# Six weight slots instead of five, combine weights turned behind the expert loop, and logits in two bank pairs

## The reference

```python
def _L0_ffn_ref(x, phi, scale, w1, b1, w2, b2):
    xn = _l2norm(x, axis=2)
    phin = scale * _l2norm(phi, axis=0)
    logits = jnp.einsum('bmd,dnp->bmnp', xn, phin)
    d = jax.nn.softmax(logits, axis=1)
    b_, m_, n_, p_ = logits.shape
    c = jax.nn.softmax(logits.reshape(b_, m_, n_ * p_), axis=-1).reshape(b_, m_, n_, p_)
    xs = jnp.einsum('bmd,bmnp->bnpd', xn, d)
    h = jax.nn.gelu(jnp.einsum('bnpd,ndh->bnph', xs, w1) + b1[None, :, None, :], approximate=False)
    ys = jnp.einsum('bnph,nhd->bnpd', h, w2) + b2[None, :, None, :]
    y = jnp.einsum('bnpd,bmnp->bmd', ys, c)
    return y
```

## Time and profile before

| | us |
|---|---|
| time before, median of 3 runs | 987.24 (986.78 to 992.46) |
| profiled execution, its own time | 988.6 |
| span of the profile, first to last instruction | 986.7 |
| TensorE busy (matmul) | 863.3 |
| VectorE busy | 454.2 |
| ScalarE busy | 316.0 |
| GpSimd busy | 280.2 |

### The profile page before, as it was taken

One profiled execution on the slowest core, in us unless ns is written; L12 is line 12 of the kernel. 1 busy time (PEld: TensorE's weight loads), 2 busy tenths in 40 slices (PEclk: granted clock), 3 DMA queues, 4 the chain that ended last, 5 costly groups with the idle time before them and its releaser, 6 DMA issues. The chain is left out here.

```text
span 986.7 us, 17884 instructions
## 1 busy us (share of the span) xinstructions
PE 863.3 (87%) x6209; PEld 631.3 (64%) x6209; DVE 454.2 (46%) x1520; ACT 316.0 (32%) x904; POOL 280.2 (28%) x242
## 2 busy tenths in 40 slices
PE   6899999889999999884997999977465999999991
PEld 6787878666556656553854777757463666666661
DVE  6764565538633333221655688836782222222220
ACT  2544434127533323221032566633101221221210
POOL 1540000000000000000233355530018488888444
PEclk9999999779899999997997899975555999999996
DMA  8999000000069999987500000001105344455222
GB/s 265 274 337 378 1 2 2 1 1 1 2 260 422 420 421 421 420 341 171 179 15 1 1 2 0 1 1 38 39 14 149 78 105 99 92 105 105 40 24 25
DMA packets 60311, 129.52 MB, mean 131 GB/s; under 512 B 26350, under 2 KB 42336, under 8 KB 50640
## 3 DMA queue, kind: packets, MB, share of 16 engines
q1 hardware_dynamic: 30288, 119.20, 33.6%
q0 software_dynamic: 29952, 9.36, 6.9%
HBM read 116.35 MB, written 11.98 MB: 130 GB/s over the span
## 5 line engine op out<-in xcount | busy, mean ns | idle before, releaser
L1806 POOL DMA_INDIRECT out_dram<-yr,put x48 | 105.7, 2203 | 58.8 <-issue 36.0
L1261 POOL MEMSET xg<- 96x74 f32 x1 | 0.2, 157 | 412.0 <-PE bank L1234 412.0
L1870 PE MATMUL bank<-zTa,w 128*128 128x372 f32 x256 | 90.4, 497 | 0.8 <-DVE zTb L1944 0.8
L1793 POOL DMA_INDIRECT zr<-z_rows,take x48 | 66.7, 1389 | 85.7 <-issue 85.7
L1953 DVE TENSOR_TENSOR hT<-sg,bank 128x372 f32<-128x372 f32 x64 | 31.8, 538 | 108.1 <-ACT sg L1914 63.1
L1177 PE MATMUL bank<-w2s,eg 128*64 128x192 f32 x768 | 69.4, 330 | 5.7 <-ACT cT L1088 5.7
L1870 PEld LDWEIGHTS bank<-zTa,w 128*128 128x128 f32 x256 | 47.5, 194 | 38.2 <-ACT sg L1914 8.4
L1109 DVE COPY eh<-bank 128x384 f32<-128x384 f32 x32 | 17.8, 557 | 107.7 <-PE bank L1153 107.7
L1884 PE MATMUL bank<-w2r,hT 128*124 128x192 f32 x384 | 66.1, 329 | 0.8 <-DVE hT L1953 0.8
L1177 PEld LDWEIGHTS bank<-w2s,eg 128*64 128x64 f32 x768 | 56.2, 137 | 14.2 <-issue 11.5
L1914 ACT ACTIVATE sg<-bank 128x372 f32<-128x372 f32 x64 | 27.3, 478 | 116.0 <-PE bank L1875 116.0
(11 more groups left out here) (287 smaller groups left out, 1727.3 us busy)
## 6 DMA issues: line engine op xcount, KB each, us to landing
w1s<-in_w_dram SPq DMA_DIRECT2D x32, 1152.0 KB, 12.8
w2s<-in_w_dram SPq DMA_DIRECT2D x32, 1152.0 KB, 13.7
w<-in_w_dram SPq DMA_DIRECT2D x8, 1024.0 KB, 8.2
xt<-in_x_dram SPq DMA_DIRECT2D x22, 336.0 KB, 8.0
xT<-in_xT_dram SPq DMA_DIRECT2D x22, 333.0 KB, 7.3
ys<-eo SPq DMA_DIRECT2D x64, 48.0 KB, 9.6
w2r<-in_w2r_dram SPq DMA_DIRECT2D x8, 384.0 KB, 4.1
w1s<-ys SPq DMA_DIRECT2D x6, 432.0 KB, 8.6
```

What stands on the lines that cost most here:

```text
L1793: nc.gpsimd.indirect_dma_start(zr[b][:, j, :], None, z_rows, bass.IndirectOffsetOnAxis(ap=take[:, k:k + 1], axis=0), bounds_check=NROW - 1 ...
L1806: nc.gpsimd.indirect_dma_start(rows_out, bass.IndirectOffsetOnAxis(ap=put[:, k:k + 1], axis=0), yr[e % 2][:, j, :], None, bounds_check=OUT ...
L1870: nc.tensor.matmul(bank[to + 2 * part + half][:, 0:HS], w13[b][:, 0, at:at + 128], zTa[b][:, half * HS:(half + 1) * HS], start=True, stop= ...
```

## The change

It has six parts.

1. **Six slots** (RING = 6). Only slots 0 and 1 (EARLY = 2) lie in memory that is free from the start; slots 2 to 5 lie in two tiles `w1l` and `w2l` that take the place of attention's buffers and weights, and their first loads wait for attention's last residual (`sp.wait_ge(s_h, 2 * T)`). For that `cb` is split: attention's part stays, the rest (phi, image marks, hidden biases) is a second table `cd`, loaded right behind it.
2. **Combine weights behind the loop.** Eight buffers `cw` (CB = 8); the expert loop spreads the first eight tiles, DVE spreads the other 14 behind it. All transposes and ACT's copies stand behind the loop, in banks 0 to 3; combine's products use banks 4 to 7. `cT` lies in the memory of slots 4 and 5.
3. **Four output buffers** (EOB = 4) instead of two.
4. **Last outputs straight into combine's rows.** Pairs 0 to 26 (DIRECT = 27) are stored to `ys` as before. The outputs of pairs 27 to 31 go from `eo` straight to their places in `e1` and `e2`, six DMAs a pair, each from 21 or 22 rows of `eo` to one row of `e1` or `e2`. The rows of pairs 0 to 26 are collected from `ys` by six DMAs of 27 rows each, issued behind the direct stores of pair 28. Combine has one wait for all of them, and no groups of tiles.
5. **Images turned by one place.** Image marks are rotated so that image 63 lies where the loads of whole rows put it.
6. **Logits in two bank pairs.** Even tiles use banks 1 and 2, odd tiles 6 and 7; logits of tile t wait for the exponentials of tile t-2.

```diff
-RING = 5
-EARLY = 3
+RING = 6
+EARLY = 2
+EOB = 4
+DIRECT = 27
...
+CTN = 20
+CB = 8
...
+        w1s = [sb(f"w1s{q}", [128, 3 * HID]) for q in range(EARLY)]
+        w2s = [sb(f"w2s{q}", [128, 2, HB, ED]) for q in range(EARLY)]
...
+        w1l = sb("w1l", [128, RING - EARLY, 3 * HID])
+        w2l = sb("w2l", [128, RING - EARLY, 2, HB, ED])
...
+        e1 = w1l[:, 0:2].rearrange("p s (t d) -> p (s t) d", d=ED)
+        e2 = w2l[:, 0:2].rearrange("p s e j d -> p (s e j) d")
+        cTs = [w1l[:, 2:4].rearrange("p s n -> p (s n)"), w2l[:, 2].rearrange("p e j d -> p (e j d)")]
...
             sp.dma_start(cb[:], ins["cb"]).then_inc(s_cbi, 16)
+            sp.dma_start(cd[:], ins["cd"]).then_inc(s_cbi, 16)
             sp.dma_start(cc[:], ins["cc"]).then_inc(s_cci, 16)
...
             def logits(t, q):
                 b = q % 2
                 pe.wait_ge(s_hTc, T + t + 1)
-                if after(t, 1):
-                    pe.wait_ge(s_cce, t)
-                    pe.wait_ge(s_cdl, t)
+                if after(t, 2):
+                    pe.wait_ge(s_cce, t - 1)
+                    pe.wait_ge(s_cdl, t - 1)
                 for c in range(2):
-                    nc.tensor.matmul(bank[1][0:TP, 0:NE], hnT[b][:, c, :], phin[:, c, :], start=(c == 0), stop=(c == 1))
+                    nc.tensor.matmul(bank[1 + 5 * b][0:TP, 0:NE], hnT[b][:, c, :], phin[:, c, :], start=(c == 0), stop=(c == 1))
...
                     if s == EARLY:
-                        sp.wait_ge(s_h, T)
+                        sp.wait_ge(s_h, 2 * T)
...
                 p = s - RING
                 if p >= 0:
-                    b = p % 2
+                    b = p % EOB
                     sp.wait_ge(s_do, p + 1)
                     for e in range(2):
-                        sp.dma_start(ys_of[p + e * NPAIR], eo[b][e * B:(e + 1) * B]).then_inc(s_eo[b], 16)
-                if s == NPAIR + 1:
-                    sp.wait_ge(s_dh, NPAIR - 1)
+                        n = p + e * NPAIR
+                        if p < DIRECT:
+                            sp.dma_start(ys_of[n], eo[b][e * B:(e + 1) * B]).then_inc(s_eoo[b], 16)
+                        else:
+                            for to, lo, hi in places(n):
+                                sp.dma_start(to, eo[b][e * B + lo:e * B + hi]).then_inc(s_eoo[b], 16)
+                if p == DIRECT:
+                    sp.dma_start(e2[NE:2 * NE, 0:T], ins["b2"].rearrange("n (t d) -> n t d", d=ED)).then_inc(s_el, 16)
+                if p == DIRECT + 1:
+                    for r in range(DIRECT - EOB, DIRECT):
+                        sp.wait_ge(s_eoo[r % EOB], rows_out_by(r))
                     for k in range(2):
-                        sp.dma_start(e2[k][NE:2 * NE], ins["b2"].rearrange("n (t d) -> n t d", d=ED)).then_inc(s_b2, 16)
+                        n = slice(k * NPAIR, k * NPAIR + DIRECT)
+                        for g in range(2):
+                            to = slice(g * NE + k * NPAIR, g * NE + k * NPAIR + DIRECT)
+                            sp.dma_start(e1[to, 0:T - 1], ys_of[n, g * (T - 1):(g + 1) * (T - 1)]).then_inc(s_el, 16)
+                        sp.dma_start(e2[n, 0:T], ys_of[n, 2 * (T - 1):B]).then_inc(s_el, 16)
+
+        def places(n):
+            return ((e1[n:n + 1, 0:T - 1], 0, T - 1), (e1[NE + n:NE + n + 1, 0:T - 1], T - 1, 2 * (T - 1)), (e2[n:n + 1, 0:T], 2 * (T - 1), B))
...
-                if 1 <= s < T + 1:
-                    spread_c(s - 1)
+                if 1 <= s <= CB:
+                    spread_c(dve, s - 1)
...
-                if p < T:
-                    pe.wait_ge(s_eTa, p + 1)
-                elif p >= 2:
+                if p >= 2:
                     pe.wait_ge(s_do, p - 1)
...
+        def combine_act(act):
+            for t in range(T):
+                act.wait_ge(s_eT, t + 1)
+                nc.scalar.copy(cT(t), bank[t % 4][:, 0:2 * TP].rearrange("p (c q) -> p c q", c=2)).then_inc(s_eTa, 1)
...
         def combine_pe(pe):
-            pe.wait_ge(s_b2, 32)
+            for part in range(2):
+                pe.wait_ge(s_dc[part], NPAIR)
+
+            def transpose_c(t):
+                pe.wait_ge(s_ecw, t + 1)
+                if t >= 4:
+                    pe.wait_ge(s_eTa, t - 3)
+                spread = cw[t % CB][:].rearrange("p g n -> p (g n)")
+                nc.tensor.transpose(bank[t % 4][:, 0:TP], spread[:, 0:128], ident[0:TP, 0:TP])
+                nc.tensor.transpose(bank[t % 4][:, TP:2 * TP], spread[:, 128:4 * NE], ident[0:TP, 0:TP]).then_inc(s_eT, 1)
+
+            for t in range(T):
+                transpose_c(t)
+            pe.wait_ge(s_el, 16 * (1 + 2 * GB))
+            for b in range(EOB):
+                pe.wait_ge(s_eoo[b], rows_out_by(NPAIR - EOB + b))
+            pe.wait_ge(s_db, NPAIR)
+            pe.wait_ge(s_do, NPAIR)
+            pe.wait_ge(s_eTa, T)
```

More of the change, by code:

```diff
@@ L164, in tower @@
         open_scope()
+        colD, nD = columns(PACK_D)
+        cd = sb("cd", [128, nD])
+        Dc = {name: of(cd, colD, name) for name in colD}
+        xy = sb("xy", [128, 2, NE, B])
+        phisq = sb("phisq", [HALF, 2, NE])
+        ce = sb("ce", [TP, T, NE])
+        image = Dc["image"][:, 0:GB]
+        image_or_any = Dc["image"]
+        w1s = [sb(f"w1s{q}", [128, 3 * HID]) for q in range(EARLY)]
+        w2s = [sb(f"w2s{q}", [128, 2, HB, ED]) for q in range(EARLY)]
+        b1s = Dc["b1s"].rearrange("p (e n j) -> p e n j", e=2, n=NPAIR)
+        open_scope()
         colB, nB = columns(PACK_B)
@@ L212, in tower @@
         open_scope()
-        w1s += [sb(f"w1s{q}", [128, 3 * HID]) for q in range(EARLY, RING)]
-        w2s += [sb(f"w2s{q}", [128, 2, HB, ED]) for q in range(EARLY, RING)]
-        open_scope()
         ha = [sb(f"ha{b}", [TP, 3, 2, 64]) for b in range(2)]
@@ L231, in tower @@
         close_scope()
+        close_scope()
+        open_scope()
+        w1l = sb("w1l", [128, RING - EARLY, 3 * HID])
+        w2l = sb("w2l", [128, RING - EARLY, 2, HB, ED])
+        w1s += [w1l[:, q] for q in range(RING - EARLY)]
+        w2s += [w2l[:, q] for q in range(RING - EARLY)]
         open_scope()
@@ L409, in tower @@
         s_yc = [sem("routed_output_copied_act"), sem("routed_output_copied_dve")]
-        s_eo = [sem(f"expert_output_out{b}") for b in range(2)]
+        s_eoo = [sem(f"slot_output_out{b}") for b in range(EOB)]
         s_ph = sem("norm_constants_steps")
@@ L441, in tower @@
         s_eTa = sem("combine_weights_kept")
-        s_b2 = sem("expert_output_bias_in")
-        s_el = [sem(f"expert_rows_in{k}") for k in range(len(LOADS))]
+        s_el = sem("expert_rows_in")
         s_ey = sem("combine_product")
@@ L882, in dispatch_act @@
             act.wait_ge(s_ln, 5 + 4)
-            nc.scalar.activation(hnorm[:], hvar[:], ACT.Sqrt, scale=float(ED)).then_inc(s_cns, 1)
+            nc.scalar.activation(hnorm[:], hvar[:], ACT.Sqrt, scale=float(ED)).then_inc(s_phs, 1)
             def copy_T(t, q):
@@ L896, in exps @@
                     act.wait_ge(s_ccw, t - 1)
-                nc.scalar.activation(cexp[b][:], bank[1][0:TP, 0:NE], ACT.Exp, bias=cneg[b][:], accum_out=csum[b][:]).then_inc(s_cce, 1)
+                nc.scalar.activation(cexp[b][:], bank[1 + 5 * b][0:TP, 0:NE], ACT.Exp, bias=cneg[b][:], accum_out=csum[b][:]).then_inc(s_cce, 1)
                 act.wait_ge(s_cdl, t + 1)
@@ L906, in store @@
                     if isinstance(t, int) and t == T - 1:
-                        last = nc.scalar.copy(xy[:, c, :, B - 1:B].rearrange("p n g -> p g n"), p[:, c, 0:1])
+                        last = nc.scalar.copy(xy[:, c, :, B - 1:B].rearrange("p n g -> p g n"), p[:, c, GB - 1:GB])
                     else:
@@ L1081, in output @@
                 act.wait_ge(s_dy, p + 1)
[L1082 to L1088 removed]
+                if p >= EOB:
+                    act.wait_ge(s_eoo[p % EOB], rows_out_by(p - EOB))
+                nc.scalar.copy(eo[p % EOB][:], bank[6 + b][:, 0:ED]).then_inc(s_do, 1)
             for s in range(NPAIR + 2):
@@ L1223, in combine_pe @@
         def combine_pe(pe):
[L1224 removed]
+            for part in range(2):
[15 more added lines that the diff above has]
+            pe.wait_ge(s_eTa, T)
             def product(t):
[L1227 to L1228 removed]
                 if t >= 4:
                     pe.wait_ge(s_h, 2 * T + t - 3)
[L1231 to L1234 removed]
+                nc.tensor.matmul(bank[4 + t % 4][0:TP, 0:ED], cT(t)[:, 0], e1[:, t, :], start=True, stop=False)
+                nc.tensor.matmul(bank[4 + t % 4][0:TP, 0:ED], cT(t)[:, 1], e2[:, t, :], start=False, stop=True).then_inc(s_ey, 1)
             for t in range(T):
```

107 lines of the change are left out of this document (33 added, 74 removed).

## The result

The changed kernel takes 982.77 us (median of 20 runs, 975.87 to 988.55), the kernel before in the same comparison 990.7 us. The ratio is 0.9939, 95% interval 0.9917 to 0.9961: 0.6% faster, 6 us, where the forecast was 970 us and 17 us. The ratio leaves out executions over 1.5% above a kernel's fastest one, so it is not the quotient of the two medians. The profiled execution took 982.76 us (span 980.9), 5.8 us less in span than the one before.

The account below looks back on a forecast made before the run. It took full DMA engines to bound the experts and busy TensorE dispatch, with idle time at dispatch's start and behind the experts. 988.6 - 6.8 (dispatch) - 10.5 (gap, 5.8 of it the slot) = 971.3, on the median's scale 970 us; range 962 to 982.

Parts of the forecast that it names:

- Dispatch: Start of dispatch: two bank pairs shorten the logits' wait and keep the clock at 1.00; 6.8 us, bounds 1.8 and 6.8.
- rival 1: Start of dispatch: the clock falls all the same, only 1.8 of 6.8 us are gained; 975 us, chance 0.20.
- Six slots: Experts: one weight pair less streams through the full DMA queue, late loading costs nothing; 5.8 us.
- the gap: From last expert product through combine: combine ends at 470.1 instead of 480.6, 10.5 us, of which 5.8 are the slot.
- Turning the weights: Behind the experts: 22 ACT copies take 7.8 us, output copy and first transposes 0.4; done at 451.3.
- SP's queue: Behind the experts: 30 issues at 0.596 us take 17.9 us, at least 1.8 to land; done at 452.4.
- Rival 3: Behind the experts: SP's issues take longest and the gap gives back the slot's gain; 983.6 us, chance 0.10.
- The transfers: Behind the experts: biases 4.8 us and collecting loads 11.9 us at 223 GB/s land last, at 454.2.
- rival 2: Collecting loads: 27 partitions reach 7 of 16 parts, 184 GB/s, 14.4 us, 2.5 us more; 972.5 us, chance 0.10.
- Three lines: Before the first combine product: weight turning (451.3), SP's issues (452.4) and transfers (454.2); only the last to end counts.
- Half clock: Start of combine: after some 3 us idle the first three tiles run at half clock, 2.0 us more.

Follow-up runs that it names:

- e1: The kernel before with only the logits in two bank pairs changed; ratio to the kernel before 0.9931 (0.9887 to 0.9974).
- e2: The changed kernel without the six collecting loads; direct stores landed 2.1 us behind the last issue instead of 8.7.
- e3: The changed kernel without the 30 direct stores; 18.1 us from the collecting loads' first issue to the first combine product.
- e4: The changed kernel with 28 rows a piece instead of 27 and 24 direct stores instead of 30; 980.75 us.
- e5: e4 with the two collecting loads onto partitions 64 and above issued by ACT; loads at 184 GB/s, first product 22.0 us behind the last expert product.
- e8: The changed kernel with 29 rows a piece instead of 27; 1072.62 us.
- e10: The changed kernel with 120 more TensorE products between the last turned weight and the wait for the collecting loads; 989.92 us.
- e6: The changed kernel with all six collecting loads issued on ACT's queue, direct stores alone on SP's; 976.01 us.
- e7: e6 with 28 rows a piece and 24 direct stores; 983.2 us.

## Why the prediction was wrong

- **Dispatch** (forecast 6.8 us): right, 6.7 in the trace of the change, 6.8 (2.6 to 11.2) by time alone in e1. The granted clock stayed 1.00 through these turns, so rival 1 falls.
- **Six slots** (5.8 us): right. The experts end 12.3 us earlier; less 6.7 leaves 5.6. Measured by itself, from the first hidden product to the end of the last output, the stage took 179.1 us before and 173.2 after, 5.9 less; in e2, e3, e4, e5, e8 and e10, whose loops differ in the last pairs alone, it took 172.3 to 173.8. The first hidden product before, and after:

```profile
269.81 2.73 PE L1149 MATMUL bank<-w1s,xy 128*64 128x384 f32 x8 [0.48 <-ACT xy L907]
```

```profile
263.37 2.66 PE L1177 MATMUL bank<-w1s,xy 128*64 128x384 f32 x8 [0.48 <-ACT xy L923]
```

The late loads were through in the slices of dispatch, 40 us before that product. The slots alone weren't tried, since their memory is that of the weights now turned in the gap, so what left the loop shares in this number. That the experts ended within 0.3 us of the forecast 436.3 is luck in part: dispatch's first logits came at 195.5 to 206.7 us in the runs with the same code up to there.

- **Turning the weights** (7.8 us and 0.4): 5.6 us, from 436.57 to 442.2. Too dear, but it was not last.
- **SP's queue** (17.9 us at 0.596 us an issue): a direct store takes 0.75 us, SP also waited 3.0 us ahead of the loads for the stores that they read, for which the line had no term, and alone it ends 13.2 us behind the experts (e2), where the forecast had 452.4 - 443.1 = 9.3. Too cheap, but not last either. Rival 3 gave 983.6 us for this line, less than 1 us from the result, but by a cause that e2 rules out. (Its "6.8 us stay" is a slip: its own times, 483.8 against 480.6, leave 3.6, and 983.6 is 987.24 less 3.6.)
- **The transfers**: the step that failed. It had two faults. The prediction put the collecting loads at 223 GB/s, the rate of 64-row loads, "11.9" us; they ran at 183, and from issue to product they need 18.1 us (e3). That was the rate of rival 2, 184 GB/s, which had a chance of 0.10. (In the proportion of the two rows that it names, 223 GB/s onto 64 partitions would have made 94 onto 27; its 7 of 16 parts come from the port count that it cites.) Landing at 451.4, 14.8 us behind the experts, they would have cost 3.7 us more than the forecast's 11.1.
- The second fault is larger: "Three lines now end before the first combine product, and the last of them counts". The lines are not independent, and the line of the transfers had no term for the direct stores. The 18 direct stores of the last pairs stand in SP's queue and on the same DMA engines behind 2.65 MB of loads; when these are all but through, some 0.2 MB of small packets are still to move. Without the loads the same stores land 2.1 us behind their issue (e2), with the loads in another queue they still move behind them (e6). That is 7.2 us more (458.5 against 451.4), and together 22.0 us to the first product instead of 11.1.
- **Half clock** (2.0 us): 2.6 us (e10). Right in kind; the wait before it was 16 us, not the 3 of the forecast.

The sum: forecast 17.3 us, of which dispatch and slots gave 12.3 instead of 12.6, and the gap took 7.3 instead of giving 4.7.

## What to carry to other kernels

A maximum over lines holds only where the lines use different resources: where two of them end in the same DMA queue or engines, ask what each issue stands behind, and add. Loads of 27 rows moved 183 GB/s with a DMA share of 0.57, where 128-row loads of the weights move 420; so try one load of all 128 rows, with its rows arranged in DRAM for that, before filling a tile piece by piece. Look at the divisors of the number of rows: 27 and 28 made no difference to speak of, but 29 rows ran at a seventh of the rate of 28.

## What was not expected

- The rate of 27- and 28-row loads was nearly the same in four arrangements: 183, 184, 184 and 183 GB/s (the changed kernel, e4, e5, e6), with DMA shares of 0.57, 0.87, 0.89 and 0.57, from SP's queue or ACT's; e3 had 173 and e7 197. Busy engines did not mean faster ones. Why it is that number the runs do not settle: all these loads read `ys` in the same rows of 16 KB, and the reading side was never changed apart from the partitions written. 7 of 16 parts of the 420 GB/s of the earlier trace rows is 184. 27 or 28 rows reach seven groups of four in the way the Trainium skill counts them (page "SBUF — State Buffer", section "Door 1: The DMA port swizzle"). No load of 128 rows from `ys` was timed by itself.
- One row more, 29 instead of 28, made the kernel 92 us slower (1072.62 against 980.75 us).
- Issuing a transfer took the changed kernel's SP 0.31 to 0.51 us for a collecting load and 0.70 to 0.89 us for a direct store of 16 KB in 768-byte rows, so the smaller transfer is the dearer one to issue.
